# A layer norm with a buffer of its own, and its scaling moved behind the next query norm, in a fused transformer kernel

## What is computed

```python
x = L0(ctx, x)   # cross attention to ctx, a small MLP (128-4-128), self attention, skip sums, layer norms
x = L1(x, ctx)   # linear attention with elu features, layer norm
x = L2(x, ctx)   # x += MHA(ln(x), ln(x)); x += MHA(ln(x), ln(ctx)); x += MoE(ln(x))   16 heads, 8 experts, top 2
# L3, a decoder layer with 16 heads:
x1 = layernorm(x + self_attention(x, causal), g1, be1)
x2 = layernorm(x1 + cross_attention(x1, ctx), g2, be2)
x3 = layernorm(x2 + relu(x2 @ W1 + b1) @ W2 + b2, g3, be3)      # the output
```

## Time and profile before

| | |
|---|---|
| median of 3 runs | 2833.17 us |
| lowest and highest | 2823.28, 2837.10 us |
| the profiled execution, its time | 2817.95 us |
| the profiled execution, its span | 2815.7 us |
| mean granted PE clock over the span | 0.923 |
| busy: DVE | 1529.4 us, 54% |
| busy: ACT | 1521.5 us, 54% |
| busy: POOL | 545.7 us, 19% |

### The profile page before, as it was taken

One profiled execution on the slowest core, in us unless ns is written; L12 is line 12 of the kernel. 1 busy time (PEld: TensorE's weight loads), 2 busy tenths in 40 slices (PEclk: granted clock), 3 DMA queues, 4 the chain that ended last, 5 costly groups with the idle time before them and its releaser, 6 DMA issues. The chain is left out here.

```text
span 2815.7 us, 69952 instructions
## 1 busy us (share of the span) xinstructions
PE 2378.0 (84%) x27712; PEld 1661.4 (59%) x27712; DVE 1529.4 (54%) x4449; ACT 1521.5 (54%) x2379; POOL 545.7 (19%) x730
## 2 busy tenths in 40 slices
PE   3656989898989989898989989898989989897975
PEld 2434647575666657575666657575666657564743
DVE  3343555657465565657465565657465565635232
ACT  1324545665665565665656555665656565644442
POOL 2111112121212122121212222121212122121111
PEclk9655979999999999999999999999999999998986
DMA  2100010101010110101010110101010110110000
GB/s 113 34 16 13 22 29 19 33 24 43 23 44 24 29 33 19 33 23 44 23 44 24 29 33 19 33 23 45 23 44 24 28 32 21 33 29 17 17 20 17
DMA packets 103753, 84.22 MB, mean 30 GB/s; under 512 B 15001, under 2 KB 102682, under 8 KB 102938
## 3 DMA queue, kind: packets, MB, share of 16 engines
q1 hardware_dynamic: 103449, 79.91, 11.6%
HBM read 14.21 MB, written 4.19 MB: 7 GB/s over the span
## 5 line engine op out<-in xcount | busy, mean ns | idle before, releaser
L990 DVE TENSOR_REDUCE smax<-by_query_banks 128x8 f32<-128x616 f32 (+1 forms) x512 | 516.0, 1008 | 345.9 <-PE by_query_banks L1309 345.2
L776 ACT ACTIVATE probs<-by_key_banks 77x1024 f32<-77x1024 f32 (+1 forms) x480 | 485.4, 1011 | 160.2 <-PE by_key_banks L1332 156.6
L1246 PEld LDWEIGHTS by_key_banks<-moe_w,hid 128*128 128x128 f32 x4096 | 476.0, 192 | 14.1
L1246 PE MATMUL by_key_banks<-moe_w,hid 128*128 128x128 f32 x4096 | 483.7, 275 | 0.0
L757 ACT ACTIVATE hid<-by_query_banks,cols 128x512 f32<-128x512 f32 x512 | 335.0, 687 | 274.8 <-PE by_query_banks L1237 273.0
L1380 PE MATMUL weighed_bank<-probs,values 128*32 128x128 f32 x8192 | 356.5, 296 | 5.9 <-ACT probs L776 2.7
L1309 PE MATMUL by_query_banks<-k_int,q_int 32*128 32x128 f16 (+1 forms) x4096 | 198.2, 218 | 170.1 <-DVE smax L990 87.9
L1309 PEld LDWEIGHTS by_query_banks<-k_int,q_int 32*128 32x128 f16 x4096 | 120.6, 98 | 334.7 <-issue 215.4
L1380 PEld LDWEIGHTS weighed_bank<-probs,values 128*32 128x32 f32 x8192 | 206.7, 115 | 96.8 <-issue 44.5
L770 ACT ACTIVATE m_sb<-turned_bank 16x128 f16<-16x128 f32 x256 | 67.9, 265 | 293.9 <-PE turned_bank L1362 293.9
L1332 PE MATMUL by_key_banks<-q_int,k_int 32*128 32x128 f16 x3840 | 206.0, 230 | 9.2 <-ACT probs L776 7.0
(11 more groups left out here) (237 smaller groups left out, 3905.0 us busy)
## 6 DMA issues: line engine op xcount, KB each, us to landing
q_int<-q_nat SPq DMA_DIRECT2D x256, 128.0 KB, 2.7
k_int<-k_nat SPq DMA_DIRECT2D x128, 128.0 KB, 2.7
k_int<-k_nat SPq DMA_DIRECT2D x128, 77.0 KB, 2.3
x_tok<-in_x SPq DMA_DIRECT2D x17, 256.0 KB, 3.0
q_int<-m_sb SPq DMA_DIRECT2D x256, 4.0 KB
out<-res SPq DMA_DIRECT2D x16, 256.0 KB, 2.3
ctx_tok<-in_ctx SPq DMA_DIRECT2D x17, 154.0 KB
hid<-in_moe_w SPq DMA_DIRECT2D x1, 2048.0 KB
```

The costliest lines, as they stand in the source:

```text
L776: act.activation(probs[h % 2][0:nk], pair[0:nk], ACT.Exp, scale=DH ** -0.5)\
L990: dve.tensor_reduce(smax[h // 2 % 2][:, pair, :], scores, AX.X, ALU.max, negate=True)\
L1246: last = pe.matmul(B[e % 2][:, seq_tok(b)], hidden[e % 2][:, c, seq_tok(b)], moe_w2[:, e, c, :], start=(c == 0), stop=(c == CHUNKS - 1))
```

## The change

The norm n33 writes `last_hat`, a new buffer of 128x512 float32, instead of `hat`. DVE no longer waits for `scaled33` before it scales the query norm. The phase "result" moves in `LIGHT` from behind "n33_hat" to the end, behind "value1", and with it POOL's two operations and SP's transfer. The strings in `TURNS` are adapted so that the order of all other phases is the same on each engine.

```diff
--- before.py
+++ after.py
@@ -109,8 +109,8 @@
          "sa_norm", "sa_hat", "sa_turn", "proj0", "query0", "value0",
          "l3_turn", "proj2", "query2", "value2",
          "norm1", "sum1", "moe_norm", "moe_hat", "moe_turn", "router", "gate",
-         "norm3", "sum3", "n32_norm", "n32_hat", "n32_turn", "ffn_in", "ffn_out", "n33_norm", "n33_hat", "result",
-         "norm0", "sum0", "caq_norm", "caq_hat", "caq_turn", "proj1", "query1", "value1"]
+         "norm3", "sum3", "n32_norm", "n32_hat", "n32_turn", "ffn_in", "ffn_out", "n33_norm", "n33_hat",
+         "norm0", "sum0", "caq_norm", "caq_hat", "caq_turn", "proj1", "query1", "value1", "result"]
 LAYERS = ["ctx_turn", "v0", "x_turn", "scores0", "kv_a", "max0", "kv_b", "scores0_t", "values0", "hidden0", "cross",
           "cross_hat", "cross_turn", "scores1", "max1", "scores1_t", "values1", "x1_turn", "x1_elu", "linear",
           "l1_norm", "l1_hat"]
@@ -119,13 +119,13 @@
 TURNS = {
     "PE": "iiiiiihxlhhxxxllhlhllhhllhxlhlhllhhxhhlhhllxhhhlhlhhllhhlllhhhhxxxhhhhhhxhxhxhhhhhhxhhhhhhhhhhxh"
           "hhhhhhhxhhhhhhhhxhhhhhhhhxhhhhhhhhxhhhhhhxxxhhhhhhhhhhhhhhhxhhhhhhhhhhhxxhhhhhxhxxxhhhhhhhhhhhhh"
-          "hhxhhhhxhhhhxxxxxhhhxxxhhhhhhhhhhxhhxxxh",
+          "hhxhhhhxhhhhxxxxhhhxxxhhhhhhhhhhxhhxxxxh",
     "ACT": "iiiihxxxxhhllllhhhhllllhxlhhhlllhxhhhllhlllhhhhhhhxlllllhhhhhhhhhhhhhiixxxxxhhhxhhhhxhhhhhhhhhhh"
           "xhhhhhhhhxhhhhhhhhhhxhhhhhhxhhhhhhhhxxxxhhhhhhhhhhhhhhhhhhhhhhhhxxhhhhhhhhhhhhxxxxxhhhhhhhhhhhhh"
-          "hhhxhhhhxxxxxhhhxxxxhhhhhhhhhhhhhhxxhhxx",
+          "hhhxhhhhxxxxhhhxxxxhhhhhhhhhhhhhhxxhhxxx",
     "DVE": "lllxhhxhhhhxxxlllllllilhhhhxllhhhhhhhhilllllhhhhlllhhhhlxxxhhhhhhxxhhhhhhhhxhhxxxhhhhhhhhhhhhhhh"
           "hhhhhhhhxhhhhhhhhxxxhhhhhhhhhhhhhhhhhhhhxxhhhhhhhhxhhhhhhhhhhhhxhhhhxhhhhxxhhhhxxhhhhhhhhxxxhhhh"
-          "hhhhhhhhhhhhhhxxxxxxhhhhxxxiiihhhhhxxxhi",
+          "hhhhhhhhhhhhhhxxxxxhhhhxxxiiihhhhhxxxxhi",
     "POOL": "llllllllllxxhhhhhhhhhhhhhhhhhhhhhhhhhhhhhhhhhhhhhhhhhhhhhhhhhhhhhhhhhhhhhhhhhhhhhhhhhhhhhhhhhhhh"
           "hhhhhhhhhhhhhhhhhhhhhhhhhhhhhhhhhhhhhhhhhhhhhhhhhhhhhhhhhhhhhhhhhhhhhhhhhhhhhxxxllllllllllllxxxx"
           "xxixxxxxxxxxiiiixxxxxxxxxxxxxxxxxxxxxxxi",
@@ -358,6 +358,7 @@
 
         moments = {n: Moments(n + "_") for n in ("ctx", "x", "layers", "light")}
         hat, feat = sb("hat", [P, GROUP, D]), sb("feat", [P, N])
+        last_hat = sb("last_hat", [P, GROUP, D])
         l_hat, l_feat = sb("l_hat", [P, GROUP, D]), sb("l_feat", [P, N])
         x_sa, x_ca, x_moe = (sb(n, [P, GROUP, D]) for n in ("x_sa", "x_ca", "x_moe"))
         x_s3, x_c3, res3 = (sb(n, [P, GROUP, D]) for n in ("x_s3", "x_c3", "res3"))
@@ -492,12 +493,12 @@
                     yield from interleave(r, SELF2)
                 if r.b:
                     yield from interleave(r, SELF3)
+                if r.n:
+                    yield from interleave(r, CROSS2)
                 if r.t:
                     yield "result"
                     sp.wait_ge(S["out_ready"], at(r.t, "out_ready"))
                     sp.dma_start(out[r.t.step].rearrange("b t d -> t b d"), out_tok[:]).then_inc(S["out_stored"], 16)
-                if r.n:
-                    yield from interleave(r, CROSS2)
 
             def layers(g):
                 yield "kv_b"
@@ -633,11 +634,6 @@
                     pool.tensor_tensor(res3[:], res3[:], shifted(shift32), ALU.add).then_inc(S["res32"], 1)
                     yield "n33_norm"
                     root(r.norms["n33"], "", x)
-                    yield "result"
-                    pool.wait_ge(S["ln"], at(r.norms["n33"], "ln"))
-                    pool.tensor_tensor(out_tok[:], hat[:], row("g3"), ALU.mult).then_inc(S["scaled33"], 1)
-                    pool.wait_ge(S["scaled33"], at(r.t, "scaled33"))
-                    pool.tensor_tensor(out_tok[:], out_tok[:], row("be3"), ALU.add).then_inc(S["out_ready"], 1)
                 if r.n:
                     yield "caq_norm"
                     root(r.norms["caq"], "", x)
@@ -645,6 +641,12 @@
                     pool.wait_ge(S["ln"], at(r.norms["caq"], "ln"))
                     pool.tensor_tensor(x_ca[:], x_ca[:], row("ca_out_b"), ALU.add).then_inc(S["ca_res"], 1)
                     yield from twice(r, CROSS2)
+                if r.t:
+                    yield "result"
+                    pool.wait_ge(S["ln"], at(r.norms["n33"], "ln"))
+                    pool.tensor_tensor(out_tok[:], last_hat[:], row("g3"), ALU.mult).then_inc(S["scaled33"], 1)
+                    pool.wait_ge(S["scaled33"], at(r.t, "scaled33"))
+                    pool.tensor_tensor(out_tok[:], out_tok[:], row("be3"), ALU.add).then_inc(S["out_ready"], 1)
 
             def go(r):
                 weave("POOL", light(r), *([layers(r.n)] if r.n else []), *([inputs(r.i)] if r.i else []))
@@ -1100,7 +1102,7 @@
                     dve.wait_ge(S["ffn_sum"], at(g, "ffn_sum"))
                     measure(r.norms["n33"], "", x, lambda b: x_c3[:, b, :])
                     yield "n33_hat"
-                    scale(r.norms["n33"], "", x, lambda b: x_c3[:, b, :], lambda b: hat[:, b, :])
+                    scale(r.norms["n33"], "", x, lambda b: x_c3[:, b, :], lambda b: last_hat[:, b, :])
                 if r.n:
                     g = r.n
                     yield "sum0"
@@ -1109,8 +1111,6 @@
                     yield "caq_norm"
                     measure(r.norms["caq"], "", x, lambda b: x_ca[:, b, :])
                     yield "caq_hat"
-                    if r.t:
-                        dve.wait_ge(S["scaled33"], at(r.t, "scaled33"))
                     scale(r.norms["caq"], "", x, lambda b: x_ca[:, b, :], lambda b: hat[:, b, :])
                     yield from low_parts(r, CROSS2)
 
```

## The result

The changed kernel takes 2802.03 us (median of 4 runs, 2795.7 to 2807.83) against 2831.63 for the kernel before (4 runs, 2823.28 to 2837.1). The ratio is 0.9905, with a 95% interval of 0.988 to 0.9929: 27 us faster (20 to 34; the medians alone differ by 29.6), where 7.3 were forecast and the range ended at 2810. The profiled execution took 2807.83, its span is 2805.6, its mean PE clock 0.920.

What follows compares the result with a forecast made beforehand. TensorE's program order was taken to bound the kernel. 13 passes x 0.56 us saved = 7.3 us, subtracted from the median 2833.17, gave 2825.9, forecast 2826 (0.26%, within noise); the range was 2810 to 2838.

Steps and rivals of the forecast that it cites:

- What bounds the kernel: Whole kernel: TensorE, busy 84% of the span, sets the pace, so a microsecond counts where TensorE stands still.
- the queueing of 0.56: Query norm's root on GpSimd queues behind the result's pair; VectorE waits 2.08 instead of 1.52, so 0.56 us a pass.
- the pair's new place: GpSimd's two result operations, 2.55 us, move behind the copies; idle time of 8.80 becomes about 6.2, so covered.
- the transfer: SyncE sends the result behind the query projections' eight transfers, at about 1372, landing by 1375, before `res3`; cost 0.
- the lists of cost 0: Extra buffer, dropped `scaled33` wait, unchanged order on TensorE, ScalarE and VectorE, nothing changed outside the loop: cost 0.
- the sum: 13 passes x 0.56 = 7.3 us, subtracted from the median of 2833.17, giving 2825.9.
- Rival 1: TensorE's clock helps as well: runs come out at 2810.7 us, 0.8% faster; chance 0.20.
- Rival 2: TensorE finds another late input behind the turn, so no gain: 2833.2 us; chance 0.08.
- Rival 3: Clock turns against it: all 13 passes fall where the slowest did, losing 25.6 us: 2851.5; chance 0.05.
- Rival 4: Moved GpSimd pair holds up one VectorE operation per pass, costing 16.5 us: 2842.4; chance 0.03.

Runs made afterwards that it cites:

- e2: Changed kernel plus a GpSimd memset of 0.54 us ahead of the query norm's root in 13 passes; 2825.70 us, ratio 1.0003 to the kernel before.
- f1: Kernel before plus unread mask matmuls on TensorE at the two places where the clock falls; 2826.43 us, ratio 0.9991 to the kernel before.
- h2: Changed kernel plus about 0.5 us of TensorE idle time ahead of expert 5, waiting for a GpSimd memset; 2808.62 us, ratio 0.9925 to the kernel before.
- g2: Changed kernel plus 0.14 us of GpSimd padding ahead of the query norm's root; 2809.74 us, ratio 0.9941 to the kernel before.
- g1: Kernel before with only GpSimd's addition to x_ca moved behind the two copies; 2801.71 us, ratio 0.9908 to the kernel before.
- g3: Changed kernel plus about 1.05 us of GpSimd padding ahead of the query norm's root; 2825.37 us, ratio 1.0000 to the kernel before.
- g4: Changed kernel plus 0.53 us of unread TensorE matmuls ahead of expert 5 in 13 passes; 2810.40 us, ratio 0.9938 to the kernel before.
- h1: Changed kernel plus 0.53 us of unread TensorE matmuls ahead of the first expert in 13 passes; 2813.77 us, ratio 0.9947 to the kernel before.
- f4: Changed kernel with GpSimd's addition to x_ca also moved behind the two copies; 2794.32 us, ratio 0.9872 to the kernel before.

## Why the prediction was wrong

- **What bounds the kernel, the queueing of 0.56, the pair's new place, the transfer, the lists of cost 0:** right, within 0.03 us for the two waits. POOL's idle time behind the pair is 5.78 and not 6.2, since one operation on `skip` took 1.72 where it took 1.27 before, and the transfer left 0.3 later than counted; both were still covered. The counted 7.3 us are in the trace, as 0.42 and 0.56 in its two clean passes.
- **The step that failed** is in the sum: "the gain is a difference inside the loop that does not depend on that level, so I subtract it from the median". It took the clock's share of a pass as noise that an edit leaves alone, and so put at nothing the larger term, about 20 of the 27 us. How often and where a pass meets a fall changed with the edit. In the twelve passes of the two traces this is 9.9 us (16.6 less the 6.7 of 12 x 0.56); over the runs it shows in the granted clock, 0.915 and 0.923, and in e2, where 0.55 us of padding a pass gave back the whole gain. The 20 themselves are what is left of the measured gain, and their interval is as wide as its own (13 to 27).
- **Rival 1** (the clock helps as well, 0.20) named the mechanism. Its time of 2810.7 was taken from the one profiled execution, as the low end of the spread, and its gain was 9 us too small. Its reason against, that nothing in the change removes the half-clock stretches, was right of the places and wrong of the number of falls there, 20 in the twelve passes before and 16 after. The Trainium skill's rule cited there ("TensorE: Matmul & The Clock Gate", "What's actually happening", activity releases the throttle) agrees with where the falls lie, behind stretches in which PE was busy for 2.56 of 3.40 us and 4.48 of 6.80, and with f1, where filling the first place ended its falls. The inference from it, that less idle time helps wherever it lies, was not borne out: h2 added 0.61 us of idle time a pass and kept most of the gain.
- **Rival 2** (no gain) is out: passes of like clock are shorter. **Rival 3** (the clock turns against it) was the same mechanism with the other sign, and g2's profiled execution, with 11 passes of 12 at the first place and 2826.14 us where its median is 2809.74, shows that it exists; no run of any kernel took longer than 2842.91, short of its 2851.5. **Rival 4** (POOL holds DVE in the new place) did not come: DVE's `ctx_phi` has the moved pair beside it where it had `skip`, and it still takes 1.22 us, with 5.28 idle behind it. That the two engines hold each other up is real, and g1 shows how much: without POOL beside it `ctx_hat` takes 1.11 us instead of 2.07. This agrees with the exclusive lock of the Trainium skill, "SBUF — State Buffer", "Who interferes with whom".

What stays open is what fixes the share of passes that meet the first fall. The runs show that length alone does not (g3, g4) and idleness does not (h2). That the length of the pass and the distances between its weak stretches decide it together was argued from the runs and is not shown: h2 came out as it said (2810 within 6), h1 did not (2825 within 6, measured 2813.8), and no run changed a distance alone.

## What to carry to other kernels

Count an edit in passes of equal granted clock first; that is where the arithmetic holds. Then look at how many passes meet a fall and at which place, because in a loop with a short weak stretch in each turn a cut of 0.4% in the length can move the time by 1% (0.56 of 158.65 us did), and the next cut may bring only its own size. Compare the profiled execution's time with the median before reading a gain out of two traces: here they would have given 10 us for 27. Where the clock has such a share, the range has to span the lengths of pass in the trace, here 155 to 160.6, and a padded kernel tells cheaply whether a gain is the edit's own.

## What was not expected of the hardware

- Passes can settle in a repeating pattern with a fall at one place: 156.9 to 157.1 us four times in the changed kernel, 156.8 four times in the rows of g1. In the kernel before no more than two passes in a row are alike (159.8 and 159.9).
- The time over the length of a pass is steep and then flat: 0.31 us of padding in 13 passes cost 19 us, and the 0.75 beyond it cost 4.
- Half clock has a price that depends on the place: about 0.45 us for each us at the first place, where PE was busy throughout, and about 0.2 at the second, where it waited for others in between (estimates from the changed kernel's passes).
- A GpSimd addition beside VectorE's scaling of 77x128 tiles made VectorE's four operations take 2.07 us instead of 1.11, and moving it away shortened the clean pass by 0.72 (f4 against the changed kernel).
